# Probabilities times values: upper parts against both parts of a block in one 512-column product

## The reference

```
x = X
n = layernorm(x)
Q, K, V = xpos(n @ W_Q), xpos(n @ W_K, downscale), n @ W_V
p = softmax(Q K^T) * 0.9 ** |i - j|        # the decay comes after the softmax
x = x + p @ V
n = layernorm(x)
h = silu(fp4(n) @ fp4(w_gate)^T) * (fp4(n) @ fp4(w_up)^T)   # 704 wide
out = x + fp4(h) @ fp4(w_down)^T
```

## Time and profile before

| | us |
|---|---|
| three runs, median | 2568.86 |
| lowest, highest | 2558.15, 2568.91 |
| the profiled execution | 2566.71 |
| its span, first to last instruction | 2564.0 |
| TensorE busy | 2532.1 (99%) |
| VectorE busy | 2147.4 (84%) |
| GpSimd busy | 1816.0 (71%) |
| ScalarE busy | 1504.2 (59%) |
| granted TensorE clock, mean share | 0.997 |

### The profile page before, as it was taken

One profiled execution on the slowest core, in us unless ns is written; L12 is line 12 of the kernel. 1 busy time (PEld: TensorE's weight loads), 2 busy tenths in 40 slices (PEclk: granted clock), 3 DMA queues, 4 the chain that ended last, 5 costly groups with the idle time before them and its releaser, 6 DMA issues.

```text
span 2564.0 us, 51984 instructions
## 1 busy us (share of the span) xinstructions
PE 2532.1 (99%) x16188; PEld 2292.5 (89%) x16188; DVE 2147.4 (84%) x4785; ACT 1504.2 (59%) x2966; POOL 1816.0 (71%) x1918
## 2 busy tenths in 40 slices
PE   8999999999999999999999999999999999999997
PEld 7888879999999899999999999999999999999997
DVE  8999878888888888888888888888888888888886
ACT  5666555556655665666565655565556655665654
POOL 6999956667666677667766776767666776676665
PEclk9999999999999999999999999999999999999999
DMA  8777511112111311131112211131113111211110
GB/s 285 278 282 286 193 55 30 37 56 96 32 46 35 109 38 46 32 106 44 42 34 69 83 40 38 42 108 37 42 35 104 42 42 34 90 62 40 38 38 21
DMA packets 163473, 203.27 MB, mean 79 GB/s; under 512 B 15184, under 2 KB 116752, under 8 KB 163216
## 3 DMA queue, kind: packets, MB, share of 16 engines
q1 hardware_dynamic: 163216, 200.01, 24.1%
HBM read 103.42 MB, written 77.59 MB: 71 GB/s over the span
## 4 chain that ended last, share of the span: by engine, by line
PE 82%; DMA 1%; POOL 1%; issue 1%; DVE 1%; SPq 0%; ACT 0%; POOLq 0%; DVEq 0%; ACTq 0%
PE score L488 26%; PE acc L623 19%; PE ring L488 18%; PE acc L488 8%; PE ring L591 6%; PE ring L643 3%; PE ring L582 1%; PE acc L665 1%; DMA keys<-k_dram 1%; SPq L419 0%; ACT probs L791 0%; POOL h_buf L976 0%; POOL h_buf L970 0%; POOL hq_buf L983 0%; POOL probs L955 0%
## 5 line engine op out<-in xcount | busy, mean ns | idle before, releaser
L488 PE MATMUL score<-keys,q_st 128*128 128x512 f32 x3072 | 757.8, 395 | 4.4 <-ACT probs L791 2.6
L488 PEld LDWEIGHTS score<-keys,q_st 128*128 128x128 f32 x3072 | 558.1, 188 | 113.1 <-issue 3.0
L623 PE MATMUL acc<-vals,pT 128*128 128x256 f32 x3984 | 556.9, 287 | 0.8 <-DVE pT L1175 0.8
L955 POOL TENSOR_TENSOR probs<-probs,decay 128x512 f32<-128x512 f32 (+3 forms) x416 | 446.3, 1086 | 142.7 <-ACT probs L791 142.7
L488 PE MATMUL ring<-w_gu,xqT 128*128 128x512 f32 (+1 forms) x2304 | 509.0, 374 | 0.0
L623 PEld LDWEIGHTS acc<-vals,pT 128*128 128x128 f32 x3984 | 498.9, 189 | 6.1 <-DVE pT L1175 2.0
L488 PEld LDWEIGHTS ring<-w_gu,xqT 128*128 128x128 f32 x2304 | 418.7, 188 | 62.9
L761 ACT ACTIVATE pT<-ring 128x512 fp32r<-128x512 f32 (+3 forms) x432 | 226.6, 534 | 376.1 <-PE ring L591 368.3
L1188 DVE TENSOR_REDUCE smax<-score 128x1 f32<-128x1024 f32 x256 | 312.3, 1220 | 98.4 <-PE score L488 97.6
L1175 DVE TENSOR_TENSOR pT<-ring,pT 128x512 fp32r<-128x512 f32 (+3 forms) x432 | 250.9, 605 | 69.0 <-ACT pT L761 67.8
L961 POOL TENSOR_TENSOR xv<-xv,xe 128x256 f32<-128x256 f32 x128 | 94.1, 735 | 270.6 <-DVE xv L1036 270.6
(11 more groups left out here) (133 smaller groups left out, 4613.9 us busy)
## 6 DMA issues: line engine op xcount, KB each, us to landing
k_dram<-keys SPq DMA_DIRECT2D x56, 512.0 KB, 4.7
keys<-k_dram SPq DMA_DIRECT2D x56, 512.0 KB, 7.6
edge<-vals SPq DMA_DIRECT2D x288, 64.0 KB, 2.1
q_raw<-q_dram SPq DMA_DIRECT2D x129, 128.0 KB, 2.6
x_in<-X SPq DMA_DIRECT2D x32, 512.0 KB, 4.5
q_dram<-q_stage SPq DMA_DIRECT2D x32, 512.0 KB, 5.7
x_res<-X SPq DMA_DIRECT2D x128, 128.0 KB, 2.1
out<-x_res SPq DMA_DIRECT2D x128, 128.0 KB, 1.7
```

The lines of the kernel that those rows point to most:

```text
L488: mm = pe.matmul(dst, stat(a, k), mov(m, k), start=i == 0, stop=ends and i == n - 1)
L623: mm = pe.matmul(pv_out, pT[g % 2][:, a, j * P:(j + 1) * P], edge[place][:] if kb in edges else vals[m][:, kb, :], start=i == 0, stop=i == ...
L955: op = pool.tensor_tensor(probs[:, k0:k1], probs[:, k0:k1], decay[:, off + k0:off + k1], ALU.mult)
```

## The change

- The two parts of the values become one tensor `both_vals` with a part dimension, 16 KB apart in a partition. For a whole block the upper part of the probabilities is multiplied with both parts in one matmul of 512 columns, which fills both halves of `acc`; the lower part is multiplied with the upper part of the values as before, into the first half. A corner block has its two matmuls of 256 columns into the first half.
- The first matmul has to write all 512 columns, so corner blocks come last in their group, and where a first group would hold only a corner (tiles 10 and 14) it gets two blocks.
- VectorE adds the two halves of `acc` to x one after the other, the second behind a wait for the first (one more step in the chain `ln2_step`).
- The down product goes to the first 256 columns of the last score bank. It waits for both exponentials of the step instead of `x1_done`, and the fourth quarter of the next scores waits for `y_done`. The attention product no longer waits for `y_done`.
- VectorE's `result` moves from the end of its list to the place behind `h_scales(.., 0)` (L1279).
- The lower and upper parts of the transposed probabilities are tensors of their own; the lower ones stay 64 bytes off the line places, the upper ones move onto them.
- A memset ahead of the statistics of stage one (L1056) goes.

```diff
--- before.py
+++ after.py
@@ -75,6 +75,8 @@
     bs = band(t)
     size = CT if 0 < t < T - 1 else CT - 1
     first = len(bs) % size or size
+    if first == 1 and t >= BAND:
+        first = 2
     return [bs[:first]] + [bs[i:i + size] for i in range(first, len(bs), size)]
 
 
@@ -150,7 +152,8 @@
 
         ident = sb("ident", [P, P])
         keys = [sb(f"keys{i}", [P, KT, L], F32R) for i in range(2)]
-        vals = [sb(f"vals{i}", [P, T, D], F32R) for i in range(2)]
+        both_vals = sb("vals", [P, 2, T, D], F32R)
+        vals = [both_vals[:, i, :, :] for i in range(2)]
         h_buf, hq_buf = [sb(f"h_buf{i}", [P, 2 * F]) for i in range(2)], sb("hq_buf", [P, 2 * FT])
         hv, he = ([x[:, i * F:(i + 1) * F] for x in h_buf] for i in range(2))
         silu = he
@@ -202,8 +205,10 @@
         xqT = [sb(f"xqT{i}", [P, KT, P], F32R) for i in range(2)]
         gap("gap_T", 2 * UNIT, sb, 0)
         hT = [sb(f"hT{i}", [P, HK, P], F32R) for i in range(2)]
-        pT = [sb(f"pT{i}", [P, 2, CT * P], F32R) for i in range(2)]
+        pT_lo = [sb(f"pT_lo{i}", [P, CT * P], F32R) for i in range(2)]
         gap("gap_gu", 0, sb, 2 * UNIT)
+        pT_hi = [sb(f"pT_hi{i}", [P, CT * P], F32R) for i in range(2)]
+        pT = [pT_hi, pT_lo]
         w_gu = [sb(f"w_gu{i}", [P, KT, 2 * F], F32R) for i in range(2)]
         w_dn = [sb(f"w_dn{i}", [P, HK, D], F32R) for i in range(2)]
         probs = sb("probs", [P, L])
@@ -211,7 +216,7 @@
         score = ctx.enter_context(nc.psum_tensor("score", [P, 4, CH], F32))
         ring = [ctx.enter_context(nc.psum_tensor(f"ring{i}", [P, CH], F32)) for i in range(RING)]
         acc = ctx.enter_context(nc.psum_tensor("acc", [P, 2, D], F32))
-        pv_out, dn_out = acc[:, 0, :], acc[:, 1, :]
+        pv_out, dn_out = [acc[:, i, :] for i in range(2)], score[:, NC - 1, 0:D]
         t_bank = [ring[0], ring[1]]
         v_bank = [ring[2][:, :].rearrange("p (t d) -> p t d", t=2), acc[:, :, :]]
 
@@ -240,7 +245,7 @@
         xq_step, xg_ready, xq_ready = sem("xq_step"), sem("xg_ready"), sem("xq_ready")
         x_levelled, h_levelled = sem("x_levelled"), sem("h_levelled")
         hq_step, hv_ready, hg_ready, hq_ready = sem("hq_step"), sem("hv_ready"), sem("hg_ready"), sem("hq_ready")
-        NSTEP_W, NSTEP_LN2, NSTEP_XQ, NSTEP_HQ = 6, 2, 6, 5
+        NSTEP_W, NSTEP_LN2, NSTEP_XQ, NSTEP_HQ = 6, 3, 6, 5
 
 
         def later(j):
@@ -560,6 +565,8 @@
                             pe.wait_ge(exped, 2 * g - 1 + o // 2)
                     elif o == 0:
                         pe.wait_ge(exped, 2 * g)
+                    if o == NC - 1 and has(at, s - 1 - LAG):
+                        pe.wait_ge(y_done, tile(at, s - 1 - LAG) + 1)
                     mm = product(score[:, o, :], lambda a, k: q_st[s % 2][:, a, k, :],
                                  lambda m, k: keys[m][:, k, o * CH:(o + 1) * CH], range(KT))
                     if o % 2:
@@ -604,25 +611,29 @@
                     return
                 gs = groups(t % T)
                 edges = edges_at(at, t)
-                n, i = len(band(t % T)) * len(PASSES) - len(edges), 0
+
+                order = [sorted(bs, key=lambda kb: kb in edges) for bs in gs]
+                begins, ends = order[0][0], order[-1][-1]
                 batch = at[0] if t >= 0 else at[0] - 1
                 for g, bs in enumerate(gs):
                     copied(at, "pT", t, g)
                     if g == 0 and has(at, t - 1):
                         pe.wait_ge(x1_done, tile(at, t))
-                    if g == 0 and has(at, t - LAG):
-                        pe.wait_ge(y_done, tile(at, t - LAG) + 1)
                     new = [kb // VT for kb in bs if kb % VT == 0 and t == max(0, kb - BAND)]
                     if at[2] is not first_plan and new:
                         pe.wait_ge(v_parted, (batch - 1) * NV + new[-1] + 1)
-                    for j, kb in enumerate(bs):
+                    for kb in order[g]:
+                        j = kb - bs[0]
+                        hi, lo = (x[g % 2][:, j * P:(j + 1) * P] for x in pT)
                         if kb in edges:
                             place, loads = edges[kb]
                             pe.wait_ge(edge_loaded[place], loads * 32)
-                        for a, m in ((0, 0), (1, 0)) if kb in edges else PASSES:
-                            mm = pe.matmul(pv_out, pT[g % 2][:, a, j * P:(j + 1) * P], edge[place][:] if kb in edges else vals[m][:, kb, :],
-                                           start=i == 0, stop=i == n - 1)
-                            i += 1
+                            pe.matmul(pv_out[0], hi, edge[place][:], start=False, stop=False)
+                            mm = pe.matmul(pv_out[0], lo, edge[place][:], start=False, stop=kb == ends)
+                        else:
+
+                            pe.matmul(acc[:, :, :], hi, both_vals[:, :, kb, :], start=kb == begins, stop=False)
+                            mm = pe.matmul(pv_out[0], lo, vals[0][:, kb, :], start=False, stop=kb == ends)
                     if g == len(gs) - 1:
                         mm.then_inc(pv_done, 1)
                     if g == 0:
@@ -656,10 +667,10 @@
                     copied(at, "hT", t, 1)
                     if t == 0 and at[2] is first_plan:
                         pe.wait_ge(w_doubled, 16)
-                    if has(at, t - 1):
+
+                    pe.wait_ge(exped, 2 * tile(at, min(t + LAG, T - 1)) + 2)
+                    if t + LAG >= T:
                         pe.wait_ge(y_done, tile(at, t))
-                    if has(at, t + LAG - 1):
-                        pe.wait_ge(x1_done, tile(at, t + LAG - 1) + 1)
                     product(dn_out, lambda a, k: hT[a][:, k, :], lambda m, k: w_dn[m][:, k, :], range(HK - 1), False)
                     for a in range(2):
                         mm = pe.matmul(dn_out, hT[a][:, HK - 1, :], w_dn[0][:, HK - 1, :], start=False, stop=a == 1)
@@ -774,7 +785,7 @@
 
                 for g in gs:
                     n = len(groups(t % T)[g]) * P
-                    upper(pT[g % 2][:, 0, 0:n], bank(at, "pT", t, g)[:, 0:n], at, "pT", t, g)
+                    upper(pT_hi[g % 2][:, 0:n], bank(at, "pT", t, g)[:, 0:n], at, "pT", t, g)
 
             def h_transposed(at, t):
                 if has(at, t):
@@ -1053,7 +1064,6 @@
                 dve.wait_ge(ln1_stat, g * (2 * CT) + CT)
                 if c > 1 or not isinstance(i, int) or i:
                     dve.wait_ge(xn_ready, g - 1)
-                dve.memset(aggr_pad[:], 0.0)
                 for t in range(CT):
                     dve.bn_aggr(mv1[c % 2][:, t, 0:2], st1[:, t, :]).then_inc(ln1_stat, 1)
                 dve.wait_ge(ln1_stat, g * (2 * CT) + 2 * CT)
@@ -1198,7 +1208,7 @@
             def attend(at, t, gs):
                 for g in gs:
                     n = len(groups(t % T)[g]) * P
-                    lower(pT[g % 2][:, 1, 0:n], bank(at, "pT", t, g)[:, 0:n], pT[g % 2][:, 0, 0:n], at, "pT", t, g)
+                    lower(pT_lo[g % 2][:, 0:n], bank(at, "pT", t, g)[:, 0:n], pT_hi[g % 2][:, 0:n], at, "pT", t, g)
 
             def h_transposed(at, t, h):
                 if has(at, t):
@@ -1217,7 +1227,9 @@
                 dve.wait_ge(pv_done, g + 1)
                 batch = at[0] if t >= 0 else at[0] - 1
                 dve.wait_ge(res_loaded[t % XR], (batch * (T // XR) + t % T // XR) * 16 + 16)
-                dve.scalar_tensor_tensor(x1, pv_out, rinv[:, 0:1], x1, ALU.mult, ALU.add).then_inc(x1_done, 1)
+                then(dve.scalar_tensor_tensor(x1, pv_out[0], rinv[:, 0:1], x1, ALU.mult, ALU.add))
+                wait()
+                dve.scalar_tensor_tensor(x1, pv_out[1], rinv[:, 0:1], x1, ALU.mult, ALU.add).then_inc(x1_done, 1)
                 dve.wait_ge(x1_done, g + 1)
                 then(dve.bn_stats(st2[:], x1))
                 wait()
@@ -1310,8 +1322,13 @@
                 h_levels(at, s - 3)
                 residual(at, s - 1)
                 x_scales(at, s - 1, lambda p: h_made(at, s - 2, p))
-                x_levels(at, s - 1, lambda i: h_scales(at, s - 2, i))
-                result(at, s - LAG)
+
+                def meanwhile(i):
+                    h_scales(at, s - 2, i)
+                    if i == 0:
+                        result(at, s - LAG)
+
+                x_levels(at, s - 1, meanwhile)
 
             for s in range(T):
                 step(first, s)
```

## The result

The changed kernel takes 2582.0 us (median of 5 runs, 2577.7 to 2584.0) against 2568.9 us (median of 5, 2558.2 to 2570.2): ratio 1.0056, interval 1.0042 to 1.0069. It is slower by 13 us. The forecast was 2562, its range ended at 2578. The profiled execution took 2582.0 us (span 2580.2), 15.3 more than before's 2566.7.

What follows compares the result with a forecast made beforehand. TensorE, busy almost throughout and paid by the column, was taken to bound the kernel. From the profiled 2566.7 us, less 5.3 for the product and 0.5 for memsets, plus 1 for waits, came 2562 us; range 2549 to 2578.

Steps and rivals of the forecast that it cites:

- The product, -5.3 us: Product with the values: a block goes from 351 to 347 ns, gaining 4 ns on each of 1328 blocks.
- This can only act through the spacings, whose bounds hold it: Weights of the probabilities' upper parts lie 64 bytes off the lower ones' place; listed under small parts, no term of its own.
- Two new waits, +1: TensorE's down product and scores' fourth quarter wait anew with time to spare; 0 to 2 us for interruptions, taken as 1.
- VectorE's second sum, 0: The sum with x1 takes 0.52 us more, 128 times, absorbed mostly by VectorE's silu wait; 0, bound 1.6 us.
- the 55 to 60 forecast: Sign named beforehand: VectorE busy some 55 to 60 us more in the loop.
- Rival 3: VectorE becomes the one that stops TensorE, at group 0's lower parts: 2588 us, chance 0.10.
- The result's move up: VectorE's result behind L1279's maximum delays x's levels by 0.41 us, 0.2 left; next scores' maximum starts no later.
- The sum itself: The profiled 2566.7 - 5.3 (product) - 0.5 (memsets) + 1 (waits) = 2561.9, say 2562 us.
- What I named as proof against it: Wrong if TensorE idles over 5 us in the loop, wide spacing leaves 220 to 238 ns, or group 0 waits beyond tile 7.
- the rivals: Alternation removes the surplus (0.20), wide matmul dearer (0.12), VectorE stops TensorE (0.10), wide matmul costs little over its load (0.03).

Runs made afterwards that it cites:

- a0d128: Changed kernel with TensorE's loop code at a 16 KB block's start and VectorE's 128 instructions behind one; 2566.7 us as cited in a later run's expectation.
- a100_oldpT: Changed kernel with three narrow products, no second sum, edge blocks last, both probability parts in one tensor, TensorE's loop code at offset 100; 2572.3 us.
- b_al192: Kernel before the change, with only TensorE's loop code moved to 192 instructions behind a 16 KB block's start; ratio interval 1.0121 to 1.0158.
- a0d128_pT: Changed kernel, both engines' code padded (TensorE 0, VectorE 128), transposed probabilities' parts as halves of one tensor, wide product kept; 2579.3 us (1.0035 to 1.0063).

## Why the prediction was wrong

- *The product, -5.3 us.* The spacings came as forecast: 230.4 ns behind a wide matmul and 118 behind a narrow one, in the mean, against 117.0 for the old narrow ones (the first matmul of a run of them apart, which is some 85 ns longer in both kernels). Yet 84 steps without a stall take 17.694 us against 17.695: the term came to 0.1 us in 128 steps. The product itself gained 0.015 us a step, and scores, gate and up lost nearly as much.
- *"This can only act through the spacings, whose bounds hold it"*: here the places of the two parts were set to nothing. They act through the spacings, as it says, but by as much as the product's term: for narrow matmuls the new places are dearer by 0.041 us a step, 5.2 us, and for the wide product cheaper by 0.038. Taken with narrow matmuls, the places cost 5.2 us and the wide form gives 6.3; taken at before's places, the wide form costs 3.7 us and the new places give 4.9; up to 0.9 us go to the rest of the edit in both. Either way the forecast was 5 us too low by this.
- *Two new waits, +1.* At most 0.007 us a step, 0.9 us, is left for them. Right. The result's move up is needed: with it last, step 8 costs 0.2 us more in each batch.
- *VectorE's second sum, 0.* Right in the loop: steps 1 to 15 unchanged, the silu wait 75.4 to 19.6 us. VectorE's work grew by 69 us, more than the 55 to 60 forecast. Rival 3 did not come in the changed kernel; in five of its variants VectorE did stop TensorE in step 3, by its longer instructions. In the last five steps the sum costs 1 to 2 us (42.5 against 40.7 with the same code of TensorE), which is what a0d128 keeps over before's 40.9. In the first batch it adds to one wait (below).
- *The result's move up.* Counted as nothing gained; it lets SyncE issue the next batch's keys 0.9 us earlier, and the 1.1 us a run that before waits for them in step 0 are gone in a0d128.
- *The sum itself.* It had terms for work and for waits, none for code. This is the step that failed by most. The padding runs put that term at 2582.0 - 2567.1 = 14.9 us, more than the whole loss of 13.1, and the profiles show 12.7 of it: 8.0 in the loop (1943.1 to 1935.1) and 4.7 in the last five steps (47.2 to 42.5). VectorE's padding has 2.9 of these, TensorE's 9.8. The change shortens TensorE's loop (3915 to 3578 recorded instructions, matmuls and loads among them) and lengthens VectorE's (903 to 965), so both come to lie elsewhere; I counted instructions by what they do and not by the room they take. The 14.9 us of code and the 5.2 by which the product's term failed make the 20 us between 2562 and 2582.0. The range ended 4 us short of the result.
- *What I named as proof against it*, TensorE idle over 5 us in the loop, came true with 6.9, for a reason that none of the rivals had. That the kernel before has no stall of code in its loop is luck of its places: moving it cost 27 and 38 us.

Shown: the stalls of TensorE and those of VectorE in step 0 come and go with the place of the engine's own code, and each follows the start of a code packet of 16 KB (0.9 to 1.5 us long) at a nearly fixed distance. Not settled: VectorE's stall in the tail, which padding removes too but which has no packet on record, and which places are bad. I have no rule for those; offset 192 is free of stalls for one kernel and the worst for the other. Open is also the head. It differs by up to 7 us between profiles (first down product at 403.1 to 410.3 us), in kernels with the same code up to there. TensorE's wait for VectorE in step 4 is 2.0 us in seven of the eleven profiles with the second sum and 0.5 in the other four, 1.4 to 1.5 in three without it, and absent in before's three and in a100_oldpT: so the change seems to have a part in it, of 0.5 to 2 us, once a run; what sets its size is open.

## What to carry to other kernels

Before a few microseconds of a long loop are put down to a change, look for waits without a releaser just behind the loop's jump, at its exit and on every engine, and pad the code of both kernels to see what they are worth. Ask first whether such a wait ends with a DMA's landing or with another engine's work (the matmul's row can name what the load's row doesn't): two of the stalls that I first put down to code did. Here padding moved the changed kernel 15 us down and the kernel before 38 us up, more than the work in question. A gain of a few nanoseconds a matmul must be measured at the same places of its operands, and on steps without stalls; medians of whole runs can't show it. An experiment that takes an instruction away changes the code of its engine too, so it needs a padded control.

## What the runs showed of the hardware

- A late jump back costs 4.75 us of idle TensorE and lowers its clock for the work behind it: 6.9 us for one jump (b_al192, step 0 at 22.5 against 15.7).
- Each of the six stalls of TensorE in the loop of the changed kernel ends 2.50 to 2.66 us behind the start of a 16 KB code packet, each of the 13 in the padded kernel before 2.95 to 3.13 us, each of the 24 of VectorE in step 0 (the four runs without the sum) 3.1 to 3.4 us. Which instruction stops went with the place of the engine's own code in all 18 profiles.
- One VectorE instruction (L1048 ahead of step 3, 704 columns) takes 0.89 to 1.46 us in most batches and 1.87 in others, in one kernel both. In a0d128_pT six of seven batches have the long one, and step 3 is 1.1 us longer in each.
- 64 bytes in the place of the stationary operands change 36 narrow float32 matmuls from 4.439 to 4.483 us, 1.2 ns each, and turn the sign of what a wide one is worth: -0.049 us a step at one pair of places, +0.029 at the other.
- 512 columns with a load each cost 230.4 ns with the moving operand in two places 16 KB apart, as in one (the scores' 230).
